# First layer of a graph network on one core: bias written into PSUM by ScalarE, odd one-hot matrices built on GpSimd, and a new order of VectorE's step

## The reference

```python
h = relu(layernorm(x))
ei = concat(h[src], edge_attr_64)             # 50000 x 320
core = relu(ei @ W1 + b1) @ W2 + b2           # 50000 x 256
gate = sigmoid(ei @ Wg + bg)
msg = gate * core
agg = segment_sum(msg, dst)                   # 3125 x 256
x = x + layernorm(agg + h) * gamma + beta
```

## Time and profile before

| | us |
|---|---|
| median of three runs (lowest, highest) | 1698.13 (1695.11, 1700.46) |
| profiled execution, span | 1691.9 |
| profiled execution, its own time | not given |
| loop of the first layer, from the first steady step to its last | 111 to 797.5 |

### The profile page before, as it was taken

How to read it: one execution, slowest core, us unless ns; L and a number is a source line. 1 busy time by engine, 2 the same in 40 slices (tenths; PEclk the granted TensorE clock), 3 DMA queues, 4 the chain that set the end, 5 groups by cost and what they waited for, 6 DMA issues and landing times. The chain is left out here.

```text
span 1691.9 us, 40433 instructions
## 1 busy us (share of the span) xinstructions
PE 1511.9 (89%) x10735; PEld 1378.6 (81%) x10735; DVE 1469.6 (87%) x3257; ACT 1202.7 (71%) x2896; POOL 1036.2 (61%) x1093
## 2 busy tenths in 40 slices
PE   6879999999999999999669688999998999999874
PEld 3669999999999999999459567787787887777653
DVE  4559999999999999999577689999999999999866
ACT  1458888888888888888056367777776767777573
POOL 0446666666666666664176577777777777777316
PEclk9989999999999999999979899999999999999888
DMA  4356666666666666665125787777777777777813
GB/s 135 138 184 186 187 186 186 186 187 186 187 187 188 185 188 185 187 184 145 33 82 191 221 245 220 231 228 231 227 228 224 225 229 227 229 226 223 281 46 97
DMA packets 164893, 318.92 MB, mean 188 GB/s; under 512 B 30231, under 2 KB 103928, under 8 KB 164436
## 3 DMA queue, kind: packets, MB, share of 16 engines
q0 software_dynamic: 66560, 219.06, 44.8%
q1 hardware_dynamic: 98132, 97.49, 18.7%
HBM read 291.90 MB, written 24.53 MB: 187 GB/s over the span
## 5 line engine op out<-in xcount | busy, mean ns | idle before, releaser
L493 POOL DMA_INDIRECT gath<-edge_in_tab,idx x392 | 413.6, 1055 | 270.5 <-DVE gate_in L933 207.6
L1226 PE MATMUL bank<-weighted,hot 128*128 128x260 f32 x880 | 238.6, 395 | 30.7 <-ACT hot L749 29.6
L506 POOL DMA_INDIRECT kept_more<-kv_tab,idx x176 | 195.5, 1111 | 60.6 <-issue 39.3
L1226 PE MATMUL bank<-w_lo,relu_hi 128*128 128x256 f32 x784 | 221.8, 283 | 0.0
L1226 PE MATMUL bank<-w_hi,relu_lo 128*128 128x256 f32 x784 | 221.7, 283 | 0.0
L1226 PE MATMUL bank<-w_hi,relu_hi 128*128 128x256 f32 x784 | 221.1, 282 | 0.0
L1226 PEld LDWEIGHTS bank<-weighted,hot 128*128 128x128 f32 x880 | 153.2, 192 | 53.4 <-ACT hot L749 36.7
L644 ACT ACTIVATE relu_hi<-bank 128x512 fp32r<-128x512 f32 x196 | 117.4, 599 | 81.4 <-PE bank L1226 81.4
L506 POOL DMA_INDIRECT hs<-kv_tab,idx x132 | 148.1, 1122 | 41.3 <-issue 36.3
L506 POOL DMA_INDIRECT xs<-kv_tab,idx x132 | 141.0, 1068 | 48.7 <-issue 22.7
L1229 PE MATMUL bank<-ident,gath 128*128 128x128 f32 x784 | 150.1, 273 | 10.6 <-DMA gath<-edge_in_tab,idx 10.6
(11 more groups left out here) (284 smaller groups left out, 4924.4 us busy)
## 6 DMA issues: line engine op xcount, KB each, us to landing
block_row<-row_tab SPq DMA_DIRECT2D x440, 64.0 KB
ea_in<-in_ea SPq DMA_DIRECT2D x392, 64.0 KB, 2.4
edge_in_tab<-node_row SPq DMA_DIRECT2D x26, 256.0 KB, 2.0
kv_tab<-qkv_row SPq DMA_DIRECT2D x25, 258.0 KB, 2.5
gath<-edge_in_tab,idx POOLq DMA_INDIRECT x392
xs<-in_x SPq DMA_DIRECT2D x1, 3328.0 KB, 15.2
v_in<-kv_tab SPq DMA_DIRECT2D x25, 130.0 KB, 2.1
rows_tab<-hs SPq DMA_DIRECT2D x25, 128.0 KB, 2.4
```

The source lines that it names most:

```text
L493: g.indirect_dma_start(gath[:, q, i, :], None, edge_in_tab, bass.IndirectOffsetOnAxis(ap=idx[:, half, q, i:i + 1], axis=0)).then_inc(gath_ ...
L506: g.indirect_dma_start(kept(u, 0, KVW)[:, i, :], None, kv_tab, bass.IndirectOffsetOnAxis(ap=idx1[:, half, u % BATCH, i:i + 1], axis=0)).th ...
L1226: return nc.tensor.matmul(out_, lhsT=lhs, rhs=rhs, start=start, stop=stop)
```

## The change

1. **Bias in PSUM.** `core` loses its two bias matmuls, and its products now all accumulate (`start=False`) onto what lies in the bank. A new ScalarE stage `seed(n)` writes the bias there before: a copy of `b2_rows` (the bias on all partitions, twice side by side, loaded by two transfers where there was one) to bank 4 + n % 2, once `message` has read the chunk two before. `core` waits for it.
2. **Odd one-hot matrices on GpSimd.** ScalarE makes distances and the one-hot for even blocks only. GpSimd makes the odd ones (`odd_one_hot`), two compares of `iota_node` with the target column, 128x128 each, after it has issued the gathers of chunk b + 4. It waits for the sum of block b - 2, which reads the same buffer.
3. **GpSimd's loop is written out**, its copies of indices and the wait for them are gone: the gathers read their indices in `src_chunk`.
4. **VectorE's step** is now relu, gate, message, edges, low message, sum; low message handles block u - 4 (was u - 3) and sum block u - 5 (was u - 4). TensorE's `sum_messages` goes from lag 3 to 4.
5. **ScalarE's step**: `gates` comes before `high_message`, and `seed` is last.
6. In the prologue the split of the bias (a copy and a subtraction) goes. Some semaphores are merged there, without effect on the order.

The diff, cut:

```diff
-            b2_parts = sb(l0, "b2_parts", [2 * SHARES, HID], f32r)
+            b2_rows = sb(l0, "b2_rows", [P, 2, HID], f32)
...
-            sp.dma_start(b2_sb[:], b2.to_broadcast([2 * SHARES, HID])).then_inc(w_in, 16)
+            for i in range(2):
+                sp.dma_start(b2_rows[:, i, :], b2.to_broadcast([P, HID])).then_inc(w_in, 16)
...
-            def gather_node_rows(first, u, half, turn=0):
-                b, q = first + u, u % SLOTS
-                if q == 0:
-                    g.tensor_copy(idx[:, half, :, :], src_chunk[:, ds(b, SLOTS), :]).then_inc(idx_done, 1)
-                after(pool, gate_added, b - SLOTS + 1)
...
+            def gather_node_rows(c):
+                after(pool, gate_added, c - SLOTS + 1)
                 for i in range(2):
+                    g.indirect_dma_start(gath[:, c % SLOTS, i, :], None, edge_in_tab,
+                                         bass.IndirectOffsetOnAxis(ap=src_chunk[:, c, i:i + 1], axis=0)).then_inc(gath_in[c % SLOTS], 16)
+
+            def odd_one_hot(b):
+                if b % 2 == 1:
+                    after(pool, sum_ready, b - 1)
+                    for i in range(2):
+                        last = g.tensor_scalar(hot[:, 1, i, :], iota_node[:], rel_col[:, b, i:i + 1], None, ALU.is_equal)
+                    last.then_inc(pool_hot_done, 1)
...
+            chunks_and_blocks(pool, [(gather_node_rows, 0, CHUNKS), (odd_one_hot, 4, CHUNKS)])
...
-            s.copy(b2_parts[:], b2_sb[:]).then_inc(w_hi_done, 1)
...
             def one_hot(b):
-                act.wait_ge(dist_done, b + 1)
-                after(act, sum_ready, b - 1)
-                s.activation(hot[:, b % 2, :, :], dist[:, b % 2, :, :], ACT.Relu, bias=one_col[:], scale=-1.0).then_inc(hot_done, 1)
+                if b % 2 == 0:
+                    act.wait_ge(dist_done, b // 2 + 1)
+                    after(act, sum_ready, b - 1)
+                    s.activation(hot[:, 0, :, :], dist[:], ACT.Relu, bias=one_col[:], scale=-1.0).then_inc(hot_done, 1)
+
+            def seed(n):
+                if n < 2:
+                    act.wait_ge(row_ready, WPAD)
+                after(act, msg_done, n - 1)
+                s.copy(bank[4 + n % 2][:], b2_rows[:].rearrange("p i f -> p (i f)")).then_inc(seeded, 1)
 
             chunks_and_blocks(act, [(split_edges, 0, CHUNKS), (one_hot, 4, CHUNKS), (distances, 3, CHUNKS), (relu_inner, 2, CHUNKS),
-                                    (high_message, 4, CHUNKS), (gates, 3, CHUNKS)])
+                                    (gates, 3, CHUNKS), (high_message, 4, CHUNKS), (seed, 2, CHUNKS)])
...
-            v.tensor_tensor(b2_parts[SHARES:, :], b2_sb[SHARES:, :], b2_parts[SHARES:, :], ALU.subtract)
...
-            chunks_and_blocks(dve, [(message, 3, CHUNKS), (low_relu, 2, CHUNKS), (add_gate, 2, CHUNKS), (low_edges, 0, CHUNKS),
-                                    (low_message, 3, BLOCKS), (add_sums, 4, BLOCKS)])
+            chunks_and_blocks(dve, [(low_relu, 2, CHUNKS), (add_gate, 2, CHUNKS), (message, 3, CHUNKS), (low_edges, 0, CHUNKS),
+                                    (low_message, 4, BLOCKS), (add_sums, 5, BLOCKS)])
...
             def core(n):
+                pe.wait_ge(seeded, n + 1)
                 pe.wait_ge(relu_lo_done, n + 1)
                 for i in range(2):
                     to = bank[4 + n % 2][:, i * HID:(i + 1) * HID]
-                    mm(to, share[:], b2_parts[:], True, False)
...
-                pe.wait_ge(hot_done, b + 1)
+                if b % 2 == 0:
+                    pe.wait_ge(hot_done, b // 2 + 1)
+                else:
+                    pe.wait_ge(pool_hot_done, b // 2 + 1)
...
-            chunks_and_blocks(pe, [(edge_inputs, 0, CHUNKS), (sum_messages, 3, BLOCKS), (core, 1, CHUNKS)])
+            chunks_and_blocks(pe, [(edge_inputs, 0, CHUNKS), (sum_messages, 4, BLOCKS), (core, 1, CHUNKS)])
```

More of the change, by code:

```diff
@@ L240, in build @@
         d_step = sem("d_step")
-        counted, cumulated, sel_ready, rows_ready, off_ready, cols_ready, meta_ready = (
-            sem(n) for n in ("counted", "cumulated", "sel_ready", "rows_ready", "off_ready", "cols_ready", "meta_ready"))
+        lists_made, tallies_made, meta_ready = sem("lists_made"), sem("tallies_made"), sem("meta_ready")
         w_hi_done, w_lo_done, wqkv_hi_done, wqkv_lo_done, bo_hi_done, bo_lo_done = (
@@ L249, in build @@
         gath_in, ea_arrived = sems("gath_in", SLOTS), sems("ea_arrived", SLOTS)
-        idx_done, ea_hi_done, ea_lo_done, z_ready, relu_hi_done, relu_lo_done, gate_done, core_ready = (
-            sem(n) for n in ("idx_done", "ea_hi_done", "ea_lo_done", "z_ready", "relu_hi_done", "relu_lo_done",
+        ea_hi_done, ea_lo_done, z_ready, relu_hi_done, relu_lo_done, gate_done, core_ready = (
+            sem(n) for n in ("ea_hi_done", "ea_lo_done", "z_ready", "relu_hi_done", "relu_lo_done",
                              "gate_done", "core_ready"))
@@ L657, in distances @@
             def distances(b):
[L659 to L662, removed]
-            def one_hot(b):
-                act.wait_ge(dist_done, b + 1)
-                after(act, sum_ready, b - 1)
-                s.activation(hot[:, b % 2, :, :], dist[:, b % 2, :, :], ACT.Relu, bias=one_col[:], scale=-1.0).then_inc(hot_done, 1)
+                if b % 2 == 0:
+                    after(act, hot_done, b // 2)
+                    for i in range(2):
+                        last = s.activation(dist[:, i, :], iota_node[:], ACT.Square, bias=rel_col[:, ds(b, 1), i], scale=-1.0)
+                    last.then_inc(dist_done, 1)
+            def one_hot(b):
+                if b % 2 == 0:
[7 more added lines that the diff above has]
+                s.copy(bank[4 + n % 2][:], b2_rows[:].rearrange("p i f -> p (i f)")).then_inc(seeded, 1)
             chunks_and_blocks(act, [(split_edges, 0, CHUNKS), (one_hot, 4, CHUNKS), (distances, 3, CHUNKS), (relu_inner, 2, CHUNKS),
-                                    (high_message, 4, CHUNKS), (gates, 3, CHUNKS)])
+                                    (gates, 3, CHUNKS), (high_message, 4, CHUNKS), (seed, 2, CHUNKS)])
             act.wait_ge(lw_in, 3 * 16)
@@ L1232, in _ @@
             pe.wait_ge(consts, 1)
-            pe.wait_ge(counted, 2)
+            pe.wait_ge(lists_made, 2)
             mm(bank[0][0:HALF_C, 0:2], upto[:], count[:], True, False)
-            mm(bank[0][0:HALF_C, 1:2], ones_c[0:HALF_C, 0:HALF_C], count[:, 0:1], False, True).then_inc(cumulated, 1)
-            pe.wait_ge(sel_ready, 1)
+            mm(bank[0][0:HALF_C, 1:2], ones_c[0:HALF_C, 0:HALF_C], count[:, 0:1], False, True).then_inc(tallies_made, 1)
+            pe.wait_ge(lists_made, 3)
             for c in range(2):
@@ L1325, in edge_inputs, with onto @@
                 last.then_inc(gate_ready, 1)
+            def onto(out_, lhs, rhs):
+                return nc.tensor.matmul(out_, lhsT=lhs, rhs=rhs, start=False, stop=False, skip_group_check=True)
             def core(n):
+                pe.wait_ge(seeded, n + 1)
                 pe.wait_ge(relu_lo_done, n + 1)
```

45 lines of the change are left out of this document (20 added, 25 removed).

## The result

The changed kernel takes 1655.41 us (median of four runs, 1651.72 to 1661.73), the kernel before beside it 1696.72; the ratio is 0.9764, interval 0.9745 to 0.9783. Run again in two later batches it gave 0.9732 and 0.9724. The forecast was 1670 us and 28 us less; measured are 41 us less, inside the range. The profiled execution is the slowest of the four (1661.73, span 1659.9).

A forecast was written before the change was run, and what follows sets the result against it. TensorE was taken as full at 3.54 us a chunk, VectorE close behind; after, 3.31 (VectorE) + 0.02 + 0.06 = 3.39, saving 0.15 x 194 = 29 us, less 0.5: 1698.1 - 28 = 1670 us, range 1651 to 1701.

The forecast's parts named there:

- (a): TensorE in the first layer's loop: two bias matmuls gone, 0.236 us a chunk less, leaving 28 issues, 3.30 us.
- (b): ScalarE: seed copy 0.60 us added, distances and one-hot for even blocks only; 3.13 us a chunk, under TensorE's 3.30.
- hazard of the even one-hot: ScalarE: even one-hot, queued ahead of the relu, waits for the sum two blocks back; hidden, slack 0.4 us.
- (c): VectorE's new order: floor stays 3.31 us a chunk; the sum's wait through ScalarE's high message goes.
- The long steps: VectorE: about every eighth step has a sum 0.35 us later; at most 0.04 a chunk, taken as 0.02.
- (d): GpSimd: two compares every second chunk, 0.48 us each; load 5.8 of 6.6 us per two chunks, not the bound.
- (e): VectorE's edges meet GpSimd's second compare and stall 0.11 us in two chunks, 0.06 a chunk.
- the rule of the earlier trace: A VectorE operation with two SBUF inputs loses the rest of the concurrent GpSimd operation less 0.18 us.
- (f): Ends of the program: prologue -0.5 us, longer drain before the late blocks +1 us; everything after the first layer untouched.
- TensorE stays the bound: Rival, chance 0.18: the compare is short (0.29), nothing is lost; 3.31 us a chunk, 45 us less, 1653 us.
- ScalarE becomes the bound: Rival, chance 0.06: even one-hot's wait or a slow seed delays ScalarE; 3.45 us a chunk, 1680 us.
- The stall eats the gain: Rival, chance 0.12: compares of 0.55 to 0.65, or later, stall VectorE 0.4 in two chunks; 3.53, 1696 us.

The follow-up runs named there:

- the two-input kernel: Changed kernel with GpSimd's odd-block compares replaced by two 128x256 subtracts of two inputs; 1688.55 us, 0.9969 of the kernel before.
- the last variant: Changed kernel with GpSimd making the odd one-hot matrices one step later (lag 5, was 4); 1644.73 us, 0.9699 of the kernel before.

## Why the prediction held, and where it missed

The sum was 3.39 us a chunk; measured 3.32 to 3.33. That is 0.065 x 194 = 13 us, the whole of the difference between 28 and 41.

(a) Right: 28 issues of 0.118, 3.30; the run with the bias matmuls put back stays at 3.53. The products add up onto ScalarE's copy here in banks that TensorE wrote whole in the prologue and in which no matmul of the loop begins with `start=True`; no run tries a seed where that does not hold.

(b) The seed was right (0.588 for 0.60). ScalarE's work was over-counted: 3.13 for 2.89 measured. I had taken all but the one listed idle of 0.38 as work; the run with the second copy and the one with all one-hots both fit 2.9 for the changed kernel. What I took for work and was none can be read from pitches between 200 and 700 us. Before, the high message followed the relu by 0.69 in all 140 steps, each with the relu's wait for TensorE ahead of it; with the seed alone, where the relu does not wait, it follows by 0.48 in the median. And the relu followed the last distance by 0.78, of which 0.39 is the listed wait; without a wait that pitch is 0.29, so another 0.09 was lost there. Together that is 0.30, a little more than the 0.24 by which the work was over-counted. Why the high message comes 0.21 later behind a relu that has waited isn't shown; its register load would fit, as it stands between the two in the queue. The hazard of the even one-hot exists as a wait (0.87 every second chunk), and it is hidden.

(c) The floor was right to 0.01: 3.305 for 3.31, and the run with 26 matmuls shows that VectorE does bind. The cause given for the old 0.2 us, the wait for the high message, fits the shorter pitch, but my attribution was incomplete: the seed alone takes back 0.16 of that pitch's mean (0.85 to 0.69). The long steps, 0.02, are not there.

(d) Mis-sized: compares 0.73 in the mean for 0.48. Where nothing disturbs them they take 0.61; the rest is the second one's wait. GpSimd is at 6.4 of 6.65 us a pair: four gathers 3.91, idle for issue ahead of them 1.07 (0.17 and three times 0.30), compares 1.45.

(e) The step that failed, twice over, in opposite directions. Place: I let the compares follow the gathers that the gate frees, from g + 3.26. They start when the message does, since GpSimd no longer waits for the gate but only for TensorE's older sum (0.22 idle). Price: by the rule of the earlier trace rows VectorE loses the rest of GpSimd's operation less 0.18. Two undisturbed compares take 1.21, so from 400.81 they would end at 402.02, 0.63 behind the start of edges (401.39), and would cost 0.63 - 0.18 = 0.45 a pair or 0.22 a chunk: 3.31 + 0.02 + 0.22 = 3.55, the whole gain eaten. Measured is 0.05 a pair, 0.026 a chunk, where 0.11 and 0.06 were forecast. In this term the forecast came near by luck: the place was wrong to the bad side, the price to the good side, and the two nearly cancel.

Two things make the price low, and the runs show both. In the changed kernel edges start just ahead of the second compare, so that GpSimd gives way (0.24) and VectorE hardly. Where the compares start first (the run with the old orders of both engines), VectorE pays 0.19 a pair, which is still less than the rule gives. The rule came from operations of GpSimd with two SBUF inputs of 256 columns, and the run with two subtracts confirms it for them. Whether a compare holds VectorE less because it reads one tensor or because it reads fewer elements is open.
The Trainium skill (SBUF — State Buffer, "Who interferes with whom") has the ports that the two engines share as an exclusive lock, with the one that issues first holding it for its whole instruction and the later one blocked. The subtract beside edges agrees to within 0.15 us (0.46 lost of 0.60). The compares agree with it on who gives way most, but not on how long: a low message 0.08 behind a compare of 0.61 loses 0.13 and not 0.53, and a compare 0.02 behind edges of 0.45 loses 0.24 and not 0.43.

(f) Within what the profiles tell: nothing outside the loop moved by more than the two executions of the same kernel differ.

The rival "TensorE stays the bound" had the time (1653) but not the cause: it needed compares of 0.29. "ScalarE becomes the bound" is true of the version with all one-hots on ScalarE, by 0.07 a chunk. "The stall eats the gain" is, by its mechanism, the two-input kernel.

What each part is worth, in ratios to before: seed alone 0.983; seed and order 0.981; seed and split one-hots 0.986; all three 0.972 to 0.976; order and split without the seed 0.996. The parts are not additive. The seed opens 0.24 us on TensorE; order and split are worth about 1% together, and next to nothing or less one by one.

## What to carry to other kernels

Before adding work to an engine that shares SBUF with a full VectorE, place the added work beside VectorE's operations that read PSUM; one number in a lag did that here for 5 us. Where it must lie beside operations with two SBUF inputs, look which of the two starts first: here the later one gave way most. When three engines stand within 5% of each other, test the parts of a change in pairs: an order and its counterpart on the other engine can be one edit (12% slower when only VectorE's was undone). Where a wait that paced an engine is removed, its work moves to wherever the next wait lets it start: work out that place anew.

## What was not expected of the hardware

- The same compare (128x128, float32 to fp32r) takes 0.60 to 0.61 us on GpSimd undisturbed (617 ns in the last variant) and 0.28 on VectorE (48 of them for the late blocks, median 280 ns).
- Who waits depends on who is first. With the second copy on ScalarE the low message started 0.03 before the two compares; it kept 0.69 and they took 1.74 in place of 1.21:

```profile
402.65 0.69 DVE L955 TENSOR_TENSOR msg_lo<-msg,msg_hi 128x512 fp32r<-128x512 f32 x1
...
402.68 1.74 POOL L492 TENSOR_SCALAR hot<-iota_node,rel_col 128x128 fp32r<-128x128 f32 x2
```

- Writes alone cost nothing: the memset of 128x1200 (1105 ns) across edges and low message left them at 422 and 693 ns.
